# Windowed attention on one core: four score banks filled in one block, one value block, transposed probabilities in the scores' banks

## Chip, core and metric

The kernel runs on one core of a Trainium2 chip. The metric is the device time of one execution in microseconds, median of several runs. Engines: TensorE (PE, with its weight loads PEld), VectorE (DVE), ScalarE (ACT), GpSimd (POOL), and SP, which here only issues transfers.

## What is computed

A decoder layer on x of 4 x 512 tokens x 256, in float32: a gated recurrence, a mixing block over a context, and then two layers of local attention with an MLP. The change touches only the attention:

```python
h = shift_token(x)                      # second half of the features from the token before
q, k, v = split(h @ wqkv, 3)            # 8 heads of 64
q, k = rotary_xpos(l2norm(q) * qs, l2norm(k) * ksc)
sim = einsum('bhwid,bhwjd->bhwij', q * 8, [k of window before, k of own window])   # windows of 128 tokens
attn = softmax(where(mask, -max, sim))
x = x + (attn @ v) @ wo                 # then the MLP with GELU, x = x + ...
```

There are two such layers, over four sequences (batches) of 512 tokens, each of four windows. In a batch the first window has no window before it, so its keys are 128 wide and not 256.

## The kernel before, in words

The attention of a layer is a loop over 16 windows (tiles of 128 tokens), four to a batch, w = 0 to 3 their place in the batch. The loop body holds the windows w = 1, 2, 3 and the w = 0 of the next batch; the first window stands ahead of the loop, the last three behind it. It is software-pipelined by hand: while window n has its scores taken, window n - 1 is finished (prev), the keys and queries of n + 1 are transposed (one), the projections of n + 2 run (two), and the input of n + 3 is transposed (three). Each engine runs its own program in order; the only ties are semaphore waits (`wait_ge`), and the order within each engine's `window` function is the schedule.

On TensorE (`window`, L1847) the order before is: scores of head pairs 0 and 1 (`score_pairs(n, w, 0)`, L1798), transposes of the reciprocal row sums of n - 1 (L1836), projection 0 of n + 2 (queries, `qkv`, in `product`, L1509), value weighting of pairs 2 and 3 of n - 1 (L1825), scores of pairs 2 and 3, projection 1 (keys), transposes of the probabilities of pairs 0 and 1 (L1810), output projection of n - 1 (`project_o`, L1844), value weighting of pairs 0 and 1 of n, key transposes of n + 1 (L1777), projection 2 (values), query transposes (L1784), probability transposes 2, input transposes (L1754), probability transposes 3. A head pair fills the 128 rows of the array: its two heads' scores are matmuls over 64 rows each, and its two heads' values are matmuls into 64 columns each. A float32 matmul stands as two records in the trace, so four of them are "x8".

On VectorE (L986): `masked` 0 and 1 (add mask, take row maxima, L957; then the row bias, L963), rope of projection 0 (L926, L931), `normalise` (writes o_t of n - 1, L978), `norm_keys` (L946), `masked` 2 and 3, `att_residual` (adds the output projection of n - 1 into the stream, L984), rope of projection 1, reciprocal of the sums, sum of squares, low part of the input. On ScalarE (L1394): copy of the transposed row sums (L1392), square of projection 0 (L1342), exponentials of pairs 0 and 1 (L1370), square of projection 1, copies of the transposed probabilities 0 and 1 (`probs_transposed`, L1381, at w = 0 L1384), exponentials 2, key copy, exponentials 3, query copy, input copy, probability copies 2, value copy, probability copy 3.

PSUM has eight banks. Banks 0 and 1 hold projections, 2 the transposes of keys, queries and sums and the output projection, 3 the weighted values, 4 and 5 the transposed probabilities (pair i in 4 + i % 2), 6 and 7 the scores (one bank for each head of a pair, two pairs side by side). Semaphores that matter: `c_qk` (scores done), `c_tt` (maxima taken, scores read), `c_ex` (exponentials), `c_pt` (probabilities transposed), `c_pt_out` (copied out), `c_pv` (values weighted), `c_ot_out` (o_t written), `c_wo` (output projected), `c_res` (added). `transpose_k` of n + 1 writes bank 2 and so waits for `c_res` of n - 1. `probs_t` holds two pairs. `w_stage` is the landing buffer of weights, whole for the attention's weights and its first 1068 columns for the MLP's.

Of the kernel before, what the change touches and what calls it, by code (L numbers as in the profile page):

```python
# [25 lines left out]
P = 128  # L26
# [23 lines left out]
W1_GROUPS = 2 * KH - 1  # L50
BAND = 64
# [17 lines left out]
def build(nc, x, ctx_in, cols_in, rows_in, w_in, w_gate, w_out, wq, wk, wv, wo_x, pos_bias,  # L69
          w1_x, w2_x, lcols_in, qk_scale, rope, wqkv, wo_l, wm_l, out):  # L70
    with ExitStack() as ctx:
# [130 lines left out]
        probs_t = sb("probs_t", [P, 2, 4, P], stack=st_att)  # L202
        st_att.close()
# [58 lines left out]
        def _(sp):  # L262
# [28 lines left out]
            def load_att(l):  # L291
                sp.dma_start(w_stage[:, :], wqkv[l].rearrange("p k n -> p (k n)")).then_inc(wqkv_in, 16)
                if l:
                    sp.wait_ge(c_wo, l * NT)
                sp.dma_start(wo_sb[:, :, :], wo_l[l]).then_inc(wo_in, 16)
# [311 lines left out]
        def _(dve):  # L607
# [341 lines left out]
            def masked(n, w, i, first=False):  # L949

                u = 4 * n + i
                nk = 2 * P if w else P
                if not (isinstance(u, int) and u < 2):
                    dve.wait_ge(c_ex, 2 * u - 2)
                wait_alone(dve, c_qk, 2 * n + i // 2 + 1)
                for e in range(2):
                    dve.tensor_tensor_reduce(scores[:, i % 2, e, 0:nk],  # L957
                                             bank[6 + e][:, (i % 2) * 2 * P:(i % 2) * 2 * P + nk],
                                             mask[:, 2 * P - nk:2 * P], 1.0, NEG, ALU.add, ALU.max,
                                             row_max[:, w % 2, 2 * i + e:2 * i + e + 1]).then_inc(c_tt, 1)  # L960
# [208 lines left out]
        def _(act):  # L1169
# [204 lines left out]
            def probs_transposed(n, w, i):  # L1374

                u = 4 * n + i
                act.wait_ge(c_pt, u + 1)
                if not (isinstance(n, int) and n == 0 and i < 2):
                    act.wait_ge(c_pv, 2 * n + i // 2)
                if w:  # L1380
                    act.activation(probs_t[:, i % 2, :, :], bank[4 + i % 2][:, :].rearrange("p (c t) -> p c t", t=P),  # L1381
                                   ACT.Copy).then_inc(c_pt_out, 1)
                else:
                    act.activation(probs_t[:, i % 2, 0:4:2, :],  # L1384
                                   bank[4 + i % 2][:, :].rearrange("p (c t) -> p c t", t=P)[:, 0:4:2, :],
                                   ACT.Copy).then_inc(c_pt_out, 1)
# [118 lines left out]
        def _(pe):  # L1505
# [281 lines left out]
            def score_pairs(n, w, g):  # L1787

                if g == 0:
                    pe.wait_ge(c_qt, n + 1)  # L1790
                if not (isinstance(n, int) and n == 0 and g == 0):
                    pe.wait_ge(c_tt, 8 * n + 4 * g)
                k0 = max(w - 1, 0) * P
                nk = (w + 1) * P - k0
                for i in (2 * g, 2 * g + 1):
                    for e in range(2):
                        half = slice(e * DH, (e + 1) * DH)
                        ins = pe.matmul(bank[6 + e][:, (i % 2) * 2 * P:(i % 2) * 2 * P + nk], q_t[half, i, :],  # L1798
                                        k_t[half, i, k0:(w + 1) * P], start=True, stop=True)
                ins.then_inc(c_qk, 1)  # L1800

            def transpose_probs(n, w, i):
# [3 lines left out]
                if not (isinstance(n, int) and n == 0 and i < 2):  # L1806
                    pe.wait_ge(c_pt_out, u - 1)
                for e in range(2):
                    for k in range(2 if w else 1):
                        ins = pe.transpose(bank[4 + i % 2][:, (2 * e + k) * P:(2 * e + k + 1) * P],  # L1810
# [3 lines left out]
            def weigh_values(n, w, g):  # L1814

                pe.wait_ge(c_pt_out, 4 * n + 2 * g + 2)
                if g == 0:
                    pe.wait_ge(c_v, n + 1)
                    pe.wait_ge(c_ot_out, n)
                nk = 2 if w else 1  # L1820
                for i in (2 * g, 2 * g + 1):
                    for k in range(nk):
                        for e in range(2):
# [3 lines left out]
                                            probs_t[:, i % 2, 2 * e + k, :], start=(k == 0), stop=(k == nk - 1))  # L1827
# [19 lines left out]
            def window(n, w, l, prev, one, two, three):  # L1847
                score_pairs(n, w, 0)
                if prev:
                    transpose_sums(n - 1)  # L1850
                if two:
                    qkv(n + 2, (w + 2) % TT, 0)
                if prev:
                    weigh_values(n - 1, (w - 1) % TT, 1)
                score_pairs(n, w, 1)
                if two:
# [5 lines left out]
                weigh_values(n, w, 0)  # L1862
# [103 lines left out]
            for l in range(LAYERS):  # L1966
# [14 lines left out]
                weigh_values(n0 + NT - 1, TT - 1, 1)  # L1981
# [88 lines left out]
```

## Times and profile before

| | us |
|---|---|
| median of 3 runs | 1061.69 |
| lowest, highest | 1060.79, 1063.59 |
| span of the profiled execution | 1063.7 |
| TensorE busy in it | 983.9 (92%) |
| VectorE, ScalarE, GpSimd busy | 697.0, 556.5, 398.4 |
| attention windows of layer 0 / layer 1 start at | 391.8 / 730.1 |
| the MLPs behind them start at | 614 / 949 |

The span is the time from the first to the last instruction of one execution. In the views a matmul's record begins at its start; the chain of waits sets its pieces 0.07 to 0.25 us later, since it reckons by the ends. A weight load overlaps the matmul before it.

### The profile page before, as it was taken

What the parts mean: (1) busy time and instruction counts of PE and PEld (TensorE: products, weight loads), DVE (VectorE), ACT (ScalarE), POOL (GpSimd) and SP (SyncE); (2) the same over time, 40 slices, a digit from 0 to 9 for tenths busy, and PEclk for the clock granted to TensorE, in tenths of its full rate; (3) what the DMA queues carried; (4) which work ended last, traced back from release to release, by engine and by line L of the source; (5) the groups of instructions that cost most, each with busy time, mean ns of one, the idle gap of its engine ahead of it and who ended that gap; (6) DMA issues with size and microseconds to landing.
All of it is one profiled execution on the core that took longest, in us unless ns stands there. A gap on an engine that the chain in (4) does not pass through costs nothing.

```text
span 1063.7 us, 18012 instructions
## 1 busy us (share of the span) xinstructions
PE 983.9 (92%) x5720; PEld 777.0 (73%) x5720; DVE 697.0 (66%) x1814; ACT 556.5 (52%) x1217; POOL 398.4 (37%) x417
## 2 busy tenths in 40 slices
PE   5889969999999979999999799998999999989987
PEld 4768855777676857777777588886777777768876
DVE  6888476366575677777778545575777777735563
ACT  4467721404030327777777734444777777754432
POOL 4232613113130366666666300115565656510030
PEclk9889979999999999999999999999999999989999
DMA  6101012000000000000001110000000000000010
GB/s 244 64 1 60 20 40 104 1 1 0 0 0 1 1 21 2 2 22 0 21 0 32 41 60 9 0 21 1 2 22 0 21 0 24 17 12 10 1 55 25
DMA packets 14349, 25.38 MB, mean 24 GB/s; under 512 B 864, under 2 KB 11224, under 8 KB 13528
## 3 DMA queue, kind: packets, MB, share of 16 engines
q1 hardware_dynamic: 14296, 24.72, 6.9%
q8 instruction: 27, 0.44, 0.2%
q14 instruction: 26, 0.21, 0.1%
HBM read 20.53 MB, written 2.10 MB: 21 GB/s over the span
## 4 chain that ended last, share of the span: by engine, by line
PE 74%; DVE 12%; issue 6%; ACT 4%; POOL 3%; DMA 0%; POOLq 0%; DVEq 0%; ACTq 0%
PE bank L1509 32%; PE bank L1704 5%; PE bank L1798 5%; PE bank L1656 5%; PE bank L1844 5%; PE bank L1825 4%; PE bank L1917 4%; PE bank L1810 4%; PE bank L1777 2%; PE bank L1836 2%; PE bank L1667 1%; PE bank L1784 1%; DVE scores L957 1%; POOL scanned L376 1%; PE bank L1575 1%
## 5 line engine op out<-in xcount | busy, mean ns | idle before, releaser
L1370 ACT ACTIVATE probs<-scores,row_bias,q_rnorm 128x256 f32<-128x256 f32 (+1 forms) x256 | 143.7, 565 | 10.7 <-DVE row_bias L963 10.1
L957 DVE CUSTOM_DVE_ANT_0 scores<-bank,mask 128x256 f32<-128x256 f32 (+1 forms) x256 | 89.2, 385 | 20.5 <-PE bank L1798 16.1
L507 POOL TENSOR_TENSOR norms<-norms,minus_half 128x16 f32<-128x16 f32 x32 | 93.6, 2925 | 2.7
L1509 PE MATMUL bank<-wqkv_hi,x_hi 128*128 128x512 f32 x192 | 85.4, 445 | 2.5 <-DVE rot L931 1.4
L490 POOL TENSOR_TENSOR k_tok<-rot 128x512 f32<-128x512 f32 x32 | 41.2, 1287 | 101.0 <-DVE rot L931 101.0
L1509 PE MATMUL bank<-wqkv_hi,x_lo 128*128 128x512 f32 x192 | 77.0, 401 | 0.0
L1509 PE MATMUL bank<-wqkv_lo,x_hi 128*128 128x512 f32 x192 | 77.0, 401 | 0.0
L1102 DVE SCALAR_TENSOR_TENSOR hidden<-bank,lcols,hidden 128x512 f32<-128x512 f32 (+1 forms) x48 | 35.9, 749 | 60.9 <-PE bank L1509 52.8
L1798 PE MATMUL bank<-k_t,q_t 64*128 64x256 f32 (+1 forms) x512 | 66.1, 377 | 10.1 <-DVE row_max L957 8.6
L1810 PE MATMUL bank<-ident,probs 128*128 128x128 f32 x448 | 65.9, 274 | 5.2 <-ACT probs L1370 5.0
L1342 ACT ACTIVATE squares<-bank 128x512 f32<-128x512 f32 x64 | 38.3, 598 | 61.1 <-PE bank L1509 61.1
L1825 PE MATMUL bank<-probs_t,v_tok 128*64 128x128 f32 x896 | 65.2, 286 | 1.3 <-ACT probs_t L1384 1.3
L1825 PEld LDWEIGHTS bank<-probs_t,v_tok 128*64 128x64 f32 x896 | 49.3, 140 | 22.6 <-issue 20.8
L1844 PE MATMUL bank<-wo_sb,o_t 128*128 128x256 f32 x256 | 64.2, 396 | 1.7 <-DVE o_t L978 1.7
L1509 PE MATMUL bank<-t_hi,wm_hi 128*128 128x512 f32 x160 | 64.3, 402 | 0.0
L1509 PE MATMUL bank<-t_lo,wm_hi 128*128 128x512 f32 x160 | 63.6, 397 | 0.0
L1509 PE MATMUL bank<-t_hi,wm_lo 128*128 128x512 f32 x160 | 62.7, 392 | 0.0
L1810 PEld LDWEIGHTS bank<-ident,probs 128*128 128x128 f32 x448 | 52.2, 141 | 13.0 <-ACT probs L1370 7.8
L1798 PEld LDWEIGHTS bank<-k_t,q_t 64*128 64x128 f32 x512 | 41.7, 186 | 24.6 <-DVE row_max L957 11.0
L490 POOL TENSOR_TENSOR q_tok<-rot 128x512 f32<-128x512 f32 x32 | 46.7, 1459 | 33.1 <-DVE rot L931 33.1
L926 DVE TENSOR_TENSOR rot<-bank,rope_l 128x512 f32<-128x512 f32 x64 | 44.0, 687 | 23.0 <-ACT squares L1342 22.8
L1704 PE MATMUL bank<-w,ff 128*128 128x256 f32 x256 | 56.7, 379 | 0.0
(242 smaller groups left out, 2620.0 us busy)
## 6 DMA issues: line engine op xcount, KB each, us to landing
w_stage<-in_wm_l_dram SPq DMA_DIRECT2D x8, 534.0 KB, 3.5
w_stage<-in_wqkv_dram SPq DMA_DIRECT2D x2, 1536.0 KB, 7.4
out_dram<-stream SPq DMA_DIRECT2D x4, 512.0 KB, 2.9
emb<-in_ctx_dram SPq DMA_DIRECT2D x1, 1536.0 KB, 6.5
inner<-in_w_gate_dram SPq DMA_DIRECT2D x1, 1152.0 KB, 9.1
stream<-in_x_dram SPq DMA_DIRECT2D x2, 512.0 KB, 5.1
stream<-in_x_dram SPq DMA_DIRECT2D x1, 1024.0 KB, 11.5
ew<-in_pos_bias_dram SPq DMA_DIRECT2D x1, 1024.0 KB, 11.2
```

Of the source, the lines that this page charges most:

```text
L490: pool.tensor_tensor(dst[:, par, :], rot[:, 2 * i, :], rot[:, 2 * i + 1, :], ALU.add)\
L507: pool.tensor_tensor(norms[:, 2, :], norms[:, 1, :], minus_half[:, :], ALU.pow).then_inc(c_rn, 1)
L926: dve.tensor_tensor(rot[:, 2 * i, :].rearrange("p (h d) -> p h d", d=DH), src, cos, ALU.mult)\
L957: dve.tensor_tensor_reduce(scores[:, i % 2, e, 0:nk], bank[6 + e][:, (i % 2) * 2 * P:(i % 2) * 2 * P + nk], mask[:, 2 * P - nk:2 * P], 1.0 ...
L1370: act.activation(probs[:, i % 2, e, 0:nk], scores[:, i % 2, e, 0:nk], ACT.Exp, bias=row_bias[:, w % 2, h:h + 1], scale=q_rnorm[:, w, h:h + 1],
L1509: ins = pe.matmul(out, stationary, moving, start=(first and i == 0), stop=(last and i == len(terms) - 1))
L1656: ins = pe.matmul(bank[2 + (2 * m + i + 2) % 4][:, :], src[:, j, m * P:(m + 1) * P], ew_t[:, j, :], start=(j == 0), stop=(j == TT - 1))
L1704: ins = pe.matmul(bank[6 + t // 2][:, (t % 2) * D:(t % 2 + 1) * D], ff[:, k, t * P:(t + 1) * P], w_2[:, k, :], start=(k == 0), stop=(k == ...
L1798: ins = pe.matmul(bank[6 + e][:, (i % 2) * 2 * P:(i % 2) * 2 * P + nk], q_t[half, i, :], k_t[half, i, k0:(w + 1) * P], start=True, stop=True)
L1810: ins = pe.transpose(bank[4 + i % 2][:, (2 * e + k) * P:(2 * e + k + 1) * P], probs[:, i % 2, e, k * P:(k + 1) * P], ident[:, :])
L1825: ins = pe.matmul(bank[3][e * DH:(e + 1) * DH, i * P:(i + 1) * P], v_tok[:, w - nk + 1 + k, h * DH:(h + 1) * DH], probs_t[:, i % 2, 2 * e ...
L1844: ins = pe.matmul(bank[2][:, 0:D], o_t[:, k, :], wo_sb[:, k, :], start=(k == 0), stop=(k == KI - 1))
```

## The change

`score_pairs` takes all four head pairs in one block, pairs 0 and 1 into banks 6 and 7, pairs 2 and 3 into banks 4 and 5. The transposed probabilities of a pair go to one of the banks from which its scores have been read, so a scores bank is free again when ScalarE has copied them out. The value weighting of a window is one block of all four pairs, and stands in the next window behind the transposes of the row sums. `probs_t` is four deep; its second half lies in `w_stage` from column 2048 on. Projections 0 and 1 follow each other on TensorE, and ScalarE's square of projection 0 stands behind the exponentials of pairs 0 and 1. SP waits for the last value weighting before it loads `w_stage` again.

```diff
+SCORES = (6, 4)
+        probs_t_far = w_stage[:, 2 * KD * INNER:4 * KD * INNER // 2 + 2 * 4 * P].rearrange(
+            "p (i c t) -> p i c t", i=2, t=P)
+        probs_ts = [(probs_t, probs_t_far)[i // 2][:, i % 2, :, :] for i in range(KI)]
...
             def load_att(l):
+                if l:
+                    sp.wait_ge(c_pv, l * NT)
...
             def normalise(n):
-                dve.wait_ge(c_pv, 2 * n + 2)
+                dve.wait_ge(c_pv, n + 1)
...
             def probs_transposed(n, w, i):
-                if not (isinstance(n, int) and n == 0 and i < 2):
-                    act.wait_ge(c_pv, 2 * n + i // 2)
+                if not (isinstance(n, int) and n == 0):
+                    act.wait_ge(c_pv, n)
...
             def window(n, w, l, prev, one, two, three):      # ScalarE
-                if two:
-                    square(n + 2, 0)
                 exps(n, w, 0)
                 exps(n, w, 1)
                 if two:
+                    square(n + 2, 0)
                     square(n + 2, 1)
...
+            def score_pairs(n, w):
+                pe.wait_ge(c_qt, n + 1)
...
+                for i in range(KI):
+                    if i % 2 == 0 and not (isinstance(n, int) and n == 0):
+                        pe.wait_ge(c_pt_out, 4 * n - 2 + i)
...
             def transpose_probs(n, w, i):
                 pe.wait_ge(c_ex, 2 * u + 2)
-                if not (isinstance(n, int) and n == 0 and i < 2):
-                    pe.wait_ge(c_pt_out, u - 1)
+                pe.wait_ge(c_tt, 8 * n + 4 * (i // 2) + 4)
...
+            def weigh_values(n, w):
+                pe.wait_ge(c_pt_out, 4 * n + 4)
+                pe.wait_ge(c_v, n + 1)
+                pe.wait_ge(c_ot_out, n)
...
             def window(n, w, l, prev, one, two, three):      # TensorE
-                score_pairs(n, w, 0)
+                score_pairs(n, w)
                 if prev:
                     transpose_sums(n - 1)
+                    weigh_values(n - 1, (w - 1) % TT)
                 if two:
                     qkv(n + 2, (w + 2) % TT, 0)
-                if prev:
-                    weigh_values(n - 1, (w - 1) % TT, 1)
-                score_pairs(n, w, 1)
-                if two:
                     qkv(n + 2, (w + 2) % TT, 1)
                 transpose_probs(n, w, 0)
                 transpose_probs(n, w, 1)
                 if prev:
                     project_o(n - 1)
-                weigh_values(n, w, 0)
                 if one:
                     transpose_k(n + 1, (w + 1) % 2, [(c_res, n)] if prev else [])
```

## Rows read from the trace of the kernel before

**Rows 1.** The page: granted clock in 40 slices, and one transfer.
```profile
PEclk9889979999999999999999999999999999989999
...
w_stage<-in_wqkv_dram SPq DMA_DIRECT2D x2, 1536.0 KB, 7.4
```
**Rows 2.** By stretches: us, then busy time by engine, clock, DMA.
```profile
391.83:399.80 7.97, 4.51 (x24) 2.98 (x23) 5.89 (x26) 2.28 (x7) 7.63 (x7) 0.75 0.00 0
...
407.79:421.20 13.41, 13.41 (x97) 10.52 (x97) 10.36 (x33) 10.30 (x29) 7.00 (x7) 1.00 0.00 1
421.20:435.08 13.88, 13.88 (x105) 10.94 (x104) 10.02 (x33) 10.47 (x29) 8.77 (x9) 1.00 0.01 3
448.97:461.13 12.16, 11.97 (x89) 9.34 (x89) 9.40 (x33) 9.00 (x28) 8.78 (x9) 1.00 0.14 47
...
592.83:602.50 9.67, 7.83 (x70) 5.77 (x69) 7.54 (x29) 6.22 (x17) 1.71 (x3) 1.00 0.03 9
```
**Rows 3.** The chain that ended last: start, length, what (a w = 2 window).
```profile
421.27 1.06 PE bank L1798 x8
422.33 0.59 PE bank L1836 x4
...
424.33 1.02 PE bank L1825 x16
...
426.42 1.60 PE bank L1509 x6
428.01 0.87 PE bank L1810 x8
428.89 1.73 PE bank L1844 x8
...
431.64 0.59 PE bank L1777 x4
432.23 1.40 PE bank L1509 x6
433.62 0.44 PE bank L1784 x4
...
457.87 0.66 PE bank L1777 x4
...
464.23 0.59 PE bank L1825 x8
```
**Rows 4.** TensorE's timeline, cut inside the block: start, us, what.
```profile
421.52 0.60 PE L1798 MATMUL bank<-k_t,q_t 64*128 64x256 f32 x4
421.73 0.38 PE L1798 MATMUL bank<-k_t,q_t 64*128 64x256 f32 x2
...
428.72 1.89 PE L1844 MATMUL bank<-wo_sb,o_t 128*128 128x256 f32 x8
```
**Rows 5.** ScalarE's timeline: start, us, what.
```profile
422.10 0.62 ACT L1381 ACTIVATE probs_t<-bank 128x512 f32<-128x512 f32 x1
...
424.36 0.60 ACT L1342 ACTIVATE squares<-bank 128x512 f32<-128x512 f32 x1 [0.81 <-PE bank L1509]
...
426.61 0.59 ACT L1370 ACTIVATE probs<-scores,row_bias,q_rnorm 128x256 f32<-128x256 f32 x1
...
461.90 0.42 ACT L1384 ACTIVATE probs_t<-bank 128x256 f32<-128x256 f32 x1
```
**Rows 6.** VectorE's timeline: start, us, what.
```profile
426.35 0.68 DVE L978 TENSOR_TENSOR o_t<-bank,rsum_t 128x512 f32<-128x512 f32 x1
...
427.79 0.41 DVE L957 CUSTOM_DVE_ANT_0 scores<-bank,mask 128x256 f32<-128x256 f32 x1
...
429.74 0.16 DVE L963 SCALAR_TENSOR_TENSOR row_bias<-row_max,q_rnorm 128x2 f32<-128x2 f32 x1
...
455.23 0.28 DVE L957 CUSTOM_DVE_ANT_0 scores<-bank,mask 128x128 f32<-128x128 f32 x1
...
457.39 0.42 DVE L984 TENSOR_TENSOR inner<-inner,bank 128x256 f32 x1
```

More of the change, by code:

```diff
@@ L957, in masked @@
                     dve.tensor_tensor_reduce(scores[:, i % 2, e, 0:nk],
-                                             bank[6 + e][:, (i % 2) * 2 * P:(i % 2) * 2 * P + nk],
+                                             bank[SCORES[i // 2] + e][:, (i % 2) * 2 * P:(i % 2) * 2 * P + nk],
                                              mask[:, 2 * P - nk:2 * P], 1.0, NEG, ALU.add, ALU.max,
@@ L1376, in probs_transposed @@
                 u = 4 * n + i
+                src = bank[SCORES[i // 2] + i % 2][:, :].rearrange("p (c t) -> p c t", t=P)
                 act.wait_ge(c_pt, u + 1)
-                if not (isinstance(n, int) and n == 0 and i < 2):
-                    act.wait_ge(c_pv, 2 * n + i // 2)
+                if not (isinstance(n, int) and n == 0):
+                    act.wait_ge(c_pv, n)
                 if w:
-                    act.activation(probs_t[:, i % 2, :, :], bank[4 + i % 2][:, :].rearrange("p (c t) -> p c t", t=P),
-                                   ACT.Copy).then_inc(c_pt_out, 1)
-                else:
-                    act.activation(probs_t[:, i % 2, 0:4:2, :],
-                                   bank[4 + i % 2][:, :].rearrange("p (c t) -> p c t", t=P)[:, 0:4:2, :],
-                                   ACT.Copy).then_inc(c_pt_out, 1)
+                    act.activation(probs_ts[i], src, ACT.Copy).then_inc(c_pt_out, 1)
+                else:
+                    act.activation(probs_ts[i][:, 0:4:2, :], src[:, 0:4:2, :], ACT.Copy).then_inc(c_pt_out, 1)
             def sums_transposed(n):
@@ L1785, in transpose_q @@
                 ins.then_inc(c_t, 1)
[L1787 to L1792, printed above, removed]
+            def score_pairs(n, w):
+                pe.wait_ge(c_qt, n + 1)
                 k0 = max(w - 1, 0) * P
                 nk = (w + 1) * P - k0
-                for i in (2 * g, 2 * g + 1):
+                for i in range(KI):
+                    if i % 2 == 0 and not (isinstance(n, int) and n == 0):
+                        pe.wait_ge(c_pt_out, 4 * n - 2 + i)
                     for e in range(2):
                         half = slice(e * DH, (e + 1) * DH)
-                        ins = pe.matmul(bank[6 + e][:, (i % 2) * 2 * P:(i % 2) * 2 * P + nk], q_t[half, i, :],
-                                        k_t[half, i, k0:(w + 1) * P], start=True, stop=True)
-                ins.then_inc(c_qk, 1)
+                        ins = pe.matmul(bank[SCORES[i // 2] + e][:, (i % 2) * 2 * P:(i % 2) * 2 * P + nk],
+                                        q_t[half, i, :], k_t[half, i, k0:(w + 1) * P], start=True, stop=True)
+                    if i % 2:
+                        ins.then_inc(c_qk, 1)
             def transpose_probs(n, w, i):
@@ L1805, in transpose_probs @@
                 pe.wait_ge(c_ex, 2 * u + 2)
-                if not (isinstance(n, int) and n == 0 and i < 2):
-                    pe.wait_ge(c_pt_out, u - 1)
+                pe.wait_ge(c_tt, 8 * n + 4 * (i // 2) + 4)
                 for e in range(2):
                     for k in range(2 if w else 1):
-                        ins = pe.transpose(bank[4 + i % 2][:, (2 * e + k) * P:(2 * e + k + 1) * P],
+                        ins = pe.transpose(bank[SCORES[i // 2] + i % 2][:, (2 * e + k) * P:(2 * e + k + 1) * P],
                                            probs[:, i % 2, e, k * P:(k + 1) * P], ident[:, :])
                 ins.then_inc(c_pt, 1)
[L1814 to L1819, printed above, removed]
+            def weigh_values(n, w):
+                pe.wait_ge(c_pt_out, 4 * n + 4)
+                pe.wait_ge(c_v, n + 1)
+                pe.wait_ge(c_ot_out, n)
                 nk = 2 if w else 1
-                for i in (2 * g, 2 * g + 1):
+                for i in range(KI):
                     for k in range(nk):
@@ L1826, in weigh_values @@
                                             v_tok[:, w - nk + 1 + k, h * DH:(h + 1) * DH],
-                                            probs_t[:, i % 2, 2 * e + k, :], start=(k == 0), stop=(k == nk - 1))
+                                            probs_ts[i][:, 2 * e + k, :], start=(k == 0), stop=(k == nk - 1))
                 ins.then_inc(c_pv, 1)
@@ L1980, in _ @@
                 transpose_sums(n0 + NT - 1, True)
-                weigh_values(n0 + NT - 1, TT - 1, 1)
+                weigh_values(n0 + NT - 1, TT - 1)
                 project_o(n0 + NT - 1)
```

## The prediction

> **What bounds the kernel now.** I read the page first: TensorE is granted nearly its full clock through the attention slices [rows 1]. Then the view by stretches, one attention window at a time. A window is one 128-token tile, and 32 of them run, 16 per layer. In the first window of a batch of the loop (w = 1) TensorE is busy 13.41 of 13.41 us, in the next two 13.88 of 13.88, in the last (w = 0) 11.97 of 12.16 [rows 2]. VectorE and ScalarE are busy 9 to 10.5 us of the same windows [rows 2]. So the attention loop is bound by TensorE, in program order, and every other engine has three to four microseconds of slack, but their work comes in a chain with due times, and slack in the total doesn't say that a link is in time. The chain of waits confirms it: the window that starts at 421.27 is TensorE blocks laid end to end, with no other engine between them [rows 3]. Last I read the timelines of ScalarE and VectorE for when their links in that window are done [rows 5, 6]; a reorder on a full engine is decided by those times.
>
> **What the change removes on TensorE.** Scores and value weighting use half of the array's rows or columns. Entering and leaving such a block costs: the block behind one is longer than the same block behind a full-array one, transposes 0.59 against 0.44 and a projection 1.60 against 1.40 [rows 3]. Inside a scores block the second pair of matmuls starts at 421.52, 0.32 us after the first, the third at 421.73, only 0.21 after the second [rows 2, 4]. Before there are four such blocks per window in three places; after there are two.
> Scores: one block of 1.06, and four more pairs at 0.215 = 0.86, so 1.92 for 2.12. Value weighting: 16 records take 1.02 and 8 take 0.59, so 8 more cost 0.43, and 32 cost 1.02 + 2 x 0.43 = 1.88 for 2.04. The key transposes now follow a full-array block: 0.44 for 0.59. The two projections still are one of 1.60 and one of 1.40. Sum: -0.20 - 0.16 - 0.15 = **-0.50 us per window**, in the 26 windows that TensorE bounds -13 us.
> The Trainium skill (TensorEngine Tiling, Key Properties) says that changing the tiling mode drains the engine; the rows agree in kind. Its page "TensorE: Matmul & The Clock Gate" (Step-by-step, the drain) gives some 128 cycles for a drain, 53 ns at 2.4 GHz; three changes of mode fewer would by that estimate be 0.16 us per window, -4 us in all, where the rows above give -13.
>
> **What the change adds: three waits on TensorE.** I lay the new order along a window's clock, zero at its first scores matmul (421.20), with the lengths of [rows 3, 4]. A chain piece lies 0.07 behind the matmul's own start, so a block started from a wait takes 0.07 more (0.66 for the transposes at 457.87, 0.59 behind a running block).
> *First wait.* Pairs 2 and 3 now write banks 4 and 5, where the transposed probabilities of the window before lie, and wait for `c_pt_out` of its last copy. ScalarE ends that copy at 422.72 [rows 5], 1.52 into the window; it is the tail of a ScalarE queue that starts with the query copy, which the change doesn't touch. With 0.06 for the handover (an end at 457.81 releases TensorE at 457.87 [rows 3, 6]) the second half starts at 1.58 and ends at 2.71, where it would have ended at 1.99: **+0.72**. Queued behind it on TensorE is everything.
> *Second wait.* Row-sum transposes to 3.30, the value block to 5.18, the first projection to 6.78. Only then can ScalarE square it; the move of `square(n + 2, 0)` behind `exps` costs nothing by itself, for the four exponentials, 0.58 apart, are done by 6.2. Before, the square began at 3.16 (424.36) [rows 5]. VectorE's queue runs from that square to rope to `normalise`: o_t starts 1.99 behind the square's start [rows 5, 6], so at 8.80, ends 0.68 later and releases `project_o` at 9.54. TensorE is there after the second projection (1.40) and the transposes (0.87), and would end the product at 10.78; from the wait it takes 1.89 [rows 4] and ends at 11.43: **+0.65**.
> *Third wait.* Behind `project_o` stood `weigh_values(n, w, 0)`, 1.02 us, which hid the residual addition; now `transpose_k` follows at once and waits for `c_res`. `att_residual` stands in VectorE's queue behind `masked` 2 and 3, which stand behind `normalise`: masked 2 starts 1.44 behind o_t (427.79 against 426.35), the last row bias 1.95 later, the addition 0.13 behind that and takes 0.42 [rows 6]. That is 10.24, 12.19, 12.32 and 12.74, so `transpose_k` starts at 12.80 and not at 11.43, and ends at 13.46 instead of 11.87: **+1.59**.
> The rest (1.40, 0.44, 0.44, 0.22, 0.44) leads to 16.40, 16.33 for the start of the next scores. ScalarE's tail hangs on the query transposes as before, so its last copy again ends 1.5 into the next window: the waits repeat and nothing catches up. A window with w = 2 or 3 takes 16.33 for 13.88, **+2.45** (-0.50 + 0.72 + 0.65 + 1.59).
> *w = 1*, by the same steps: the last copy is half as long and ends at 462.32, 1.19 in [rows 5]; the value block is 16 records; the exponentials (from 3.5) end at 5.84 and set the square. o_t 7.83, `project_o` from 8.57 to 10.46, the addition done at 11.77, next window at 15.36 for 13.41: **+1.95**. *w = 0*: scores at half width (0.65), value block still 1.88, o_t at 8.39, `project_o` to 11.02, masked 2 at 9.81, the addition 2.16 behind it (455.23 to 457.39 [rows 6]), next window at 15.6 for 12.16: **+3.45**.
> **Sum.** A batch of four windows +1.95 + 2 x 2.45 + 3.45 = 10.3, six batches in both loops 61.8. The window w = 1 behind each loop, two in all, 3.9. In the last two windows of a layer VectorE's MLP preparation is late already; I take +0.25 each layer for w = 2 and nothing for w = 3, whose saved value block (1.02) is paid again in the doubled block behind it. The first window of a layer has no previous tile and no third wait and loses a 0.59 block: I take -1.2, with 0 and -2.5 as ends. Together 61.8 + 3.9 + 0.5 - 2.4 = **+63.8**.
> **Edits at no cost.** `load_att(1)` waits for `c_pv` before w_stage is loaded again. On SP's queue the output weights' load behind it and two shifts wait for `c_wo` in any case, which comes after `c_pv`; the staged weights are first used in the last MLP batch, tens of microseconds later. Without that cover it would cost its own 7.4 us, once [rows 1]. POOL's rope additions shift with VectorE's rope and still end ahead of their users. The transposes' new wait for `c_tt` is for maxima taken 2 us and more earlier.
> The trace doesn't show the new waits; each is bounded from below by what is structural. The first lies between 0.4 (the w = 1 copy) and 0.8. The second is between 0 (VectorE wholly in time) and 1.1 (its size in w = 0). The third is at least 0.65 (an addition of 0.42, two handovers, and the slower start from a wait) and at most 1.8. I take the values of the walk, which lie nearest to rows of the same window.
>
> **How it stands to the median.** The profiled execution spans 1063.7 us, 0.2% over the median 1061.69. So 1063.7 + 63.8 is 1127.5 there and **1125 us** for the median, 6% slower.
>
> **Rivals.**
> *The waits are covered (faster).* For it: all three fed engines are busy under 10.5 of 13.88 us. Without a wait `project_o` would be due at 8.33 (1.99 + 0.59 + 1.88 + 1.60 + 1.40 + 0.87) and `transpose_k` at 10.06. If o_t were done by 8.27 and the addition by 10.0, -0.50 x 26 would stand alone: 1048. From those two points on it is slower, and against it speaks that o_t ends 2.67 behind the start of the square, so the square would have to start by 5.60, while the projection that it reads ends at 6.06 at the earliest.
> *Only the structural waits stay.* If VectorE's masks 2 and 3 don't delay the addition, a window pays 0.72 + 0.65 - 0.50 = 0.87, over 28 windows +24: 1086. Against it: the queue order is fixed in the code.
> *The clock falls too.* TensorE's share in a window would be 13.4 of 16.33, 82%. The slowed last window of a layer has 7.83 of 9.67, 81%, at a granted clock of 1.00 [rows 2], which speaks against it. For it: in the layer's first window, with TensorE 57% busy, 7.97 us run at a mean of 0.75 [rows 2], a loss of 2.0. One such stretch in each of eight batches is 16 more, 1141; one in each of 26 windows 52 more, 1177.
> *The edit does not do what it says.* If TensorE's pairs didn't run closer in one long block, the 0.50 goes and the waits stay: 1138, inside the range.
>
> **How the numbers follow.** Forecast 0.70 (1105 to 1145, by the bounds of the waits), structural waits alone 0.12, clock 0.08, a gain 0.06, and 0.04 for an outcome between these last and no change. The range 1085 to 1150 takes in the first two and the milder clock case. A difference of 0.3% (3.2 us) is about what a measurement of this kernel can tell. Faster 0.06, same 0.02, slower 0.92.
>
> **What would show it.** In the chain of waits the windows should no longer be TensorE alone: ScalarE's probs_t copy ahead of the second half of the scores, o_t ahead of the output projection, and the residual addition ahead of the key transposes, the last the largest. Scores matmuls 2 and 3 should start 1.6 us behind the first. The window should be 16.3 and its TensorE work 13.4. Windows of 13.4 without gaps would refute it; gaps with a clock below 0.95 in the middle of the loop would be the clock's.

## The result, and the profile after

| | before | after |
|---|---|---|
| median, us | 1062.12 (1060.79 to 1063.59) | 1129.93 (1129.12 to 1130.78) |
| ratio to before | | 1.0637 [1.0622, 1.0652] |
| profiled execution's span, us | 1063.7 | 1127.4 |
| mean granted clock | 0.975 | 0.984 |

The change makes the kernel 6.4% slower, 67.8 us in the medians and 63.7 in the spans (the profiled execution of before lies 1.6 above its median, that of after 2.5 below). The forecast was 1125.

The page of after first, since it says in three lines what has changed. Section 1 is busy time by engine, section 2's line the granted clock in 40 slices, section 4 the chain that ended last, by engine.

```profile
PE 977.2 (87%) x5720; PEld 774.1 (69%) x5720; DVE 701.2 (62%) x1814; ACT 556.4 (49%) x1217; POOL 390.7 (35%) x417
...
PEclk9899899999999989999999999999999999999999
...
PE 56%; DVE 20%; ACT 10%; issue 9%; POOL 3%; DVEq 1%; DMA 0%; POOLq 0%; ACTq 0%
```

Every engine does the work that it did before. What is new is that TensorE is now only 56% of the chain, for 74% in the kernel before, and VectorE and ScalarE are 30% of it, for 16%. The clock line answers to that of [rows 1]: the 8 near its end, at the end of the second layer's attention, is gone, and behind the slice with the first windows (395 to 423 us) nothing is below 9.

The second reading is the groups of TensorE with their idle time (busy us, mean ns of one, idle before and who ended it). Each of the three lines is one wait.

```profile
L1845 PE MATMUL bank<-wo_sb,o_t 128*128 128x256 f32 x256 | 63.4, 390 | 18.7 <-DVE o_t L984 18.7
...
L1800 PE MATMUL bank<-k_t,q_t 64*128 64x256 f32 (+1 forms) x512 | 64.8, 374 | 13.3 <-ACT w_stage L1388 10.9
...
L1780 PE MATMUL bank<-ident,k_tok 128*128 128x128 f32 x128 | 21.3, 290 | 45.9 <-DVE inner L990 42.6
```

The output projection waits for o_t, the scores for the copy of the transposed probabilities (their far half lies in w_stage), and the key transposes for the residual addition, by far the longest of the three. Then the chain of one window. It is the one that begins at 421.61, w = 2, the one whose forecast stands on [rows 3]: start, length, what.

```profile
422.71 0.50 ACT w_stage L1388
...
423.26 1.14 PE bank L1800 x8
...
424.98 1.90 PE bank L1826 x32
426.88 1.60 PE bank L1512 x6
...
428.50 0.61 ACT squares L1348
...
430.57 0.60 DVE o_t L984
431.17 1.39 DVE k_tok L952
432.56 0.33 DVE scores L963
...
434.48 0.43 DVE inner L990
...
434.96 0.66 PE bank L1780 x4
```

Where [rows 3] were TensorE blocks end to end, the chain now leaves TensorE for 0.5 us at the head of the window, and from 428.48 to 434.96, where it runs through the square, rope, o_t, the keys' normalisation, two masks and the residual addition. TensorE isn't idle for all of that: it has the second projection, the probability transposes and `project_o` beside it. By stretches (us, busy time by engine, clock, DMA), windows with w = 1, 2 and 0, against [rows 2]:

```profile
405.85:421.61 15.76, 13.22 (x88) 10.23 (x88) 10.49 (x33) 10.12 (x28) 7.39 (x8) 1.00 0.01 1
421.61:438.41 16.80, 14.06 (x105) 11.09 (x104) 10.33 (x33) 10.61 (x28) 8.33 (x9) 1.00 0.01 1
...
455.18:470.77 15.59, 12.53 (x98) 9.90 (x96) 9.20 (x33) 9.12 (x28) 8.35 (x9) 1.00 0.12 37
```

The clock stays at 1.00, and a window is 2.5 to 3.1 us longer than TensorE's busy time in it. Summed from the first scores matmul of each window to that of the next, the attention windows take 72.0 us more (37.1 in layer 0, 34.9 in layer 1); the stretch from the last window of layer 0 to the first of layer 1 takes 3.5 less (133.8 for 137.3), the rest behind the last window 2.7 less, and the first scores start 2.1 sooner. That is 63.7, the difference of the spans.

### The profile page after: what moved, and what is told of

Read it like the earlier page. It is cut to its first block, busy times and chain, and to the rows that moved or that the text cites. A ratio compares the mean times of both kernels' runs of the same rounds, so it can differ in the third digit from the quotient of the medians.

```text
span 1127.4 us, 17962 instructions
## 1 busy us (share of the span) xinstructions
PE 977.2 (87%) x5720; PEld 774.1 (69%) x5720; DVE 701.2 (62%) x1814; ACT 556.4 (49%) x1217; POOL 390.7 (35%) x417
## 4 chain that ended last, share of the span: by engine, by line
PE 56%; DVE 20%; ACT 10%; issue 9%; POOL 3%; DVEq 1%; DMA 0%; POOLq 0%; ACTq 0%
PE bank L1512 26%; PE bank L1707 5%; PE bank L1659 5%; PE bank L1914 4%; PE bank L1826 3%; DVE k_tok L952 3%; DVE scores L963 3%; ACT probs L1376 3%; PE bank L1800 3%; PE bank L1780 2%; DVE o_t L984 2%; ACT squares L1348 2%; ACT v_tok L1353 1%; DVE rot L937 1%; PE bank L1837 1%
## 5 line engine op out<-in xcount | busy, mean ns | idle before, releaser
L1512 PE MATMUL bank<-wqkv_hi,x_hi 128*128 128x512 f32 x192 | 82.3, 428 | 2.2 <-DVE rot L937 1.4
L496 POOL TENSOR_TENSOR q_tok<-rot 128x512 f32<-128x512 f32 x32 | 41.0, 1282 | 105.1 <-DVE rot L937 105.1
L1800 PE MATMUL bank<-k_t,q_t 64*128 64x256 f32 (+1 forms) x512 | 64.8, 374 | 13.3 <-ACT w_stage L1388 10.9
L1845 PEld LDWEIGHTS bank<-wo_sb,o_t 128*128 128x128 f32 x256 | 46.0, 190 | 30.3 <-DVE o_t L984 25.4
L1780 PE MATMUL bank<-ident,k_tok 128*128 128x128 f32 x128 | 21.3, 290 | 45.9 <-DVE inner L990 42.6
```

The source lines that it names most:

```text
L496: pool.tensor_tensor(dst[:, par, :], rot[:, 2 * i, :], rot[:, 2 * i + 1, :], ALU.add)\
L1512: ins = pe.matmul(out, stationary, moving, start=(first and i == 0), stop=(last and i == len(terms) - 1))
L1800: ins = pe.matmul(bank[SCORES[i // 2] + e][:, (i % 2) * 2 * P:(i % 2) * 2 * P + nk], q_t[half, i, :], k_t[half, i, k0:(w + 1) * P], start= ...
L1845: ins = pe.matmul(bank[2][:, 0:D], o_t[:, k, :], wo_sb[:, k, :], start=(k == 0), stop=(k == KI - 1))
```

## The experiments

All but the last are the kernel after with the order of a few calls changed and nothing of its computation left out. Ratios are to the kernel before. "Window" is the distance between the first scores matmuls of two windows, w = 2 and 3 unless it says otherwise: 16.8 us in the kernel after.

**The first wait, alone.** ScalarE's values copy stood between the last two probability copies.

```diff
                 probs_transposed(n, w, 2)
+                probs_transposed(n, w, 3)
                 if two:
                     values(n + 2, (w + 2) % TT)
-                probs_transposed(n, w, 3)
```

> The kernel after, with one edit: ScalarE copies the last transposed probabilities before the values, so that copy ends 0.48 us earlier (one 128x512 copy behind another). Theory of three waits: the wait of the second half of the scores (0.8 us in the trace of after) falls by 0.48 in nearly all of 30 windows, and since everything behind it on TensorE follows without slack, the time falls by 13 to 14 us, to about 1116. Rival, that the window's pace is set by VectorE's queue as a whole and a wait taken away in one place comes back in the next: the output product and the key transposes wait 0.48 longer, and the time stays at 1130.

Measured: 1118.54 us (1115.96 to 1121.04), 1.0529 [1.0508, 1.0550]. The window fell to 16.3. TensorE's timeline shows the scores as one block again (start, us, what):

```profile
434.99 2.22 PE L1800 MATMUL bank<-k_t,q_t 64*128 64x256 f32 x16
```

11 of the 68 us hung on one ScalarE copy of 0.6 us in the wrong place, where 13 to 14 were expected. In this profile the stretch behind the second layer's last window is 2.2 us longer than in that of after (135.4 for 133.2), and 3.4 us of it (992.2 to 995.6) run at a granted clock of 0.50. The block is still 2.2 and not the 1.9 of my sum; two probability copies remain behind the query copy.

**The second wait, alone.** Projection 0 goes ahead of the value block on TensorE, and its square ahead of the exponentials on ScalarE.

```diff
                     transpose_sums(n - 1)
-                    weigh_values(n - 1, (w - 1) % TT)
                 if two:
                     qkv(n + 2, (w + 2) % TT, 0)
+                if prev:
+                    weigh_values(n - 1, (w - 1) % TT)
+                if two:
                     qkv(n + 2, (w + 2) % TT, 1)
...
+                if two:
+                    square(n + 2, 0)
                 exps(n, w, 0)
                 exps(n, w, 1)
                 if two:
-                    square(n + 2, 0)
                     square(n + 2, 1)
```

> The kernel after, with projection 0 ahead of the value block on TensorE and its square ahead of the exponentials on ScalarE, as before the change; the blocks stay whole. Theory: the square starts at about 4.9 us into the window and not at 6.9, o_t is done by 7.6, ahead of the output product, so the second wait (0.65 us) goes, and the masks and the addition come 1.9 us earlier, so that the third falls to 0.6. The window goes from 16.8 to 14.9, the time to about 1080. Rival, that the exponentials, now later by 2 us, hold up the probability transposes instead: these would wait, and the gain is under half, above 1105.

Measured: 1084.31 us, 1.0201 [1.0184, 1.0219]; window 14.9, as expected, the time 4 us above what was expected. This one move takes back 46 of the 68 us, more than the second term of my sum, because VectorE's whole queue starts from that square and the third wait hangs on the same queue. The chain of a window here:

```profile
419.94 1.39 PE bank L1513 x6
421.33 1.90 PE bank L1827 x32
...
424.80 0.87 PE bank L1813 x8
425.67 1.74 PE bank L1846 x8
...
427.56 0.43 DVE inner L990
...
428.03 0.66 PE bank L1781 x4
```

`project_o` follows the probability transposes with no wait. The key transposes start 0.62 behind it, with the addition alone between them: the structural part of the third wait, for which I had 0.65.

**The third wait, from VectorE's side.** Masks 2 and 3 go ahead of rope, so that nothing but the keys' normalisation stands between o_t and the addition.

```diff
                 masked(n, w, 1)
+                masked(n, w, 2)
+                masked(n, w, 3)
                 if two:
                     rope_products(n + 2, (w + 2) % TT, 0)
...
                     norm_keys(n + 1, (w + 1) % 2)
-                masked(n, w, 2)
-                masked(n, w, 3)
```

> The kernel after, with VectorE's masks 2 and 3 moved ahead of the rope of projection 0, into the 4.3 us that it idles there. Theory: the third wait is mostly the two masks standing between o_t and the residual addition. The addition then starts when the output product ends (11.6 us into the window) and not at 12.87, the key transposes start at 12.1 and not at 13.35: 1.2 us less in each of 26 to 28 windows, 32 us in all, to about 1098; the wait left ahead of the key transposes is 0.6 to 0.7. Rival, that the addition is late because the output product itself is late: no change of the time, under 5 us.

Measured: 1115.69 us, 1.0485 [1.0463, 1.0507], 14 us below after, under half of the 32 that were expected. The direction held, the size didn't. Windows w = 2, 3 fell by 1.1 us to 15.67, down to the same structural wait, the addition alone (chain):

```profile
433.06 2.01 PE bank L1845 x8
...
435.20 0.43 DVE inner L990
...
435.68 0.65 PE bank L1780 x4
```

But w = 0 and w = 1 gained only 0.6 and 0.5, and where VectorE has the MLP preparation to do the masks come at its cost: the final w = 2 window of each layer is 1.5 longer (13.58 for 12.08), and the stretch between the layers 2.8 longer (136.5 for 133.8). Not all of the 2.8 need be the masks': 3.4 us of that stretch (635.2 to 638.6) run at a granted clock of 0.50, which the kernel after doesn't have there, and behind the second layer, at full clock, the difference is 1.8.

**The third wait, from TensorE's side.** The last projection goes between `project_o` and the key transposes, as cover for the addition, and the query transposes behind the third probability transposes.

```diff
+                if two:
+                    qkv(n + 2, (w + 2) % TT, 2)
                 if one:
                     transpose_k(n + 1, (w + 1) % 2, [(c_res, n)] if prev else [])
...
-                if two:
-                    qkv(n + 2, (w + 2) % TT, 2)
+                transpose_probs(n, w, 2)
                 if one:
                     transpose_q(n + 1, (w + 1) % 2)
-                transpose_probs(n, w, 2)
```

> The kernel after, with projection 2 moved between the output product and the key transposes, and the query transposes behind probability transposes 2. Theory: the key transposes still wait for the residual addition and start where they did (13.35 us into the window), the 1.4 us of projection 2 are inside the wait; but the key copy and the exponentials of pair 3 behind it on ScalarE are no earlier, and hold up the last probability transposes, which gives most of it back: the window falls by 0.4 to 0.7 us, the time to 1112 to 1118. Rival, that TensorE's waits alone count and what is put into one is gained whole: 1.4 us in 26 windows, 36 us, to 1094.

Measured: 1121.35 us, 1.0548 [1.0510, 1.0585]; window 16.42, 0.37 less. The 1.4 us of cover is there and is nearly all given back, as the theory had it; the gain is still smaller than its 0.4 to 0.7 and the time above its 1112 to 1118. From the chain behind the key transposes:

```profile
434.44 0.43 DVE inner L990
...
434.92 0.67 PE bank L1780 x4
...
436.11 0.89 ACT probs L1376 x3
...
439.10 0.50 ACT w_stage L1388
```

The key transposes still start at the same point of the window, since the addition ends when it did. Behind them nothing is left that TensorE could do while ScalarE goes through its tail (key copy, exponentials, query copy, x, values, probabilities), so the next scores wait for that tail. The wait that was covered on TensorE came back where ScalarE's queue ends.

**Was the keys' normalisation slowed by GpSimd?** In the window above k_tok takes 1.47 us in its own record, and masked 2 starts 1.99 behind o_t where [rows 6] have 1.44. VectorE multiplies two SBUF operands there, while GpSimd adds q_tok. In a second profile of the kernel before the same place, w = 2, reads (VectorE's and GpSimd's timeline):

```profile
427.07 0.91 DVE L946 TENSOR_TENSOR k_tok<-k_tok,norms 128x512 f32<-128x512 f32 x1
```
```profile
427.39 1.74 POOL L490 TENSOR_TENSOR q_tok<-rot 128x512 f32<-128x512 f32 x1
```

There VectorE is first and GpSimd's addition is the one that is drawn out, 1.74 for some 1.27. In the kernel after it is the other way:

```profile
430.74 1.27 POOL L496 TENSOR_TENSOR q_tok<-rot 128x512 f32<-128x512 f32 x1 [3.00 <-DVE rot L937]
```
```profile
431.08 1.47 DVE L952 TENSOR_TENSOR k_tok<-k_tok,norms 128x512 f32<-128x512 f32 x1
```

The change of order between the two engines is one of w = 2, 3 and 0. In w = 1 GpSimd was first before the change too (413.29), and VectorE drawn out. In w = 0 it was another VectorE instruction that started inside GpSimd's addition, the row bias of masks 2 (128x2, else 0.16 us). The same second profile, w = 1 and then w = 0 on both engines:

```profile
413.63 1.50 DVE L946 TENSOR_TENSOR k_tok<-k_tok,norms 128x512 f32<-128x512 f32 x1
```
```profile
455.64 1.26 POOL L490 TENSOR_TENSOR q_tok<-rot 128x512 f32<-128x512 f32 x1
```
```profile
455.87 1.05 DVE L963 SCALAR_TENSOR_TENSOR row_bias<-row_max,q_rnorm 128x2 f32<-128x2 f32 x1
```

Moving the multiplication behind the masks takes it out of that overlap:

```diff
-                if one:
-                    norm_keys(n + 1, (w + 1) % 2)
                 masked(n, w, 2)
                 masked(n, w, 3)
+                if one:
+                    norm_keys(n + 1, (w + 1) % 2)
                 if prev:
                     att_residual(n - 1, t - 1)
```

> The kernel after, with VectorE's norm_keys behind masks 2 and 3 and ahead of the residual addition. In the trace of after this product of two SBUF operands takes 1.47 us; it starts 0.34 us after GpSimd's q_tok addition and ends 0.5 us after that ends. Theory: it is held up by GpSimd's addition, alone it takes 0.68. Moved, it runs when GpSimd is idle and takes 0.68, the addition starts 0.75 us earlier in each window, and the time falls by about 20 us, to 1109. Rival, that 1.47 is what it costs wherever it stands in this order: 1.4 us again and the time stays within 5 us of 1130.

Measured: 1114.63 us, 1.0481 [1.0463, 1.0499], 15 us less where some 20 were expected; window 15.95, 0.84 less, w = 1 and w = 0 0.7 and 0.6 less; the first windows of the layers lose 2.6 and 2.4 of that again, since there the later keys are what the transposes wait for, and in the second 3.4 us (763.2 to 766.6) run at a granted clock of 0.50, which the kernel after doesn't have there. The same 32 instructions in the kernel after, grouped by form (duration ns min/median/max):

```profile
L952 DVE TENSOR_TENSOR k_tok<-k_tok,norms x32: 681/1473/1477, 382.5 to 987.8; 128x512 f32<-128x512 f32 x32
```

and in this one:

```profile
L952 DVE TENSOR_TENSOR k_tok<-k_tok,norms x32: 691/692/721, 383.3 to 976.3; 128x512 f32<-128x512 f32 x32
```

And the two engines' timelines in it:

```profile
433.37 1.27 POOL L496 TENSOR_TENSOR q_tok<-rot 128x512 f32<-128x512 f32 x1 [3.00 <-DVE rot L937]
```
```profile
433.72 0.41 DVE L963 CUSTOM_DVE_ANT_0 scores<-bank,mask 128x256 f32<-128x256 f32 x1
...
435.68 0.69 DVE L952 TENSOR_TENSOR k_tok<-k_tok,norms 128x512 f32<-128x512 f32 x1
```

Beside the same GpSimd addition (1.27 us) the masks, which read a PSUM bank, keep their 0.41, and the multiplication behind it takes 0.69. So in the kernel after 0.78 us of a k_tok was lost to GpSimd and no work; 26 of the 32 took 1.38 us or more there, and 8 of 32 in the kernel before. The Trainium skill ("SBUF — State Buffer", Who interferes with whom) says that a VectorE instruction with two SBUF inputs and a GpSimd instruction that reads SBUF contend for a port pair, and that the one issued second is blocked altogether. By that rule whichever starts second is drawn out, and the rows agree: GpSimd's 1.74 before, VectorE's 1.47 after, and the row bias's 1.05, which ends when GpSimd's addition does. VectorE's 0.91 before isn't free of it either: a GpSimd copy of 0.41 us (x_tile) had started 0.04 us ahead of it. From these rows the loss is the time that the two overlap less some 0.12 to 0.15 us: 0.78 of 0.93, 0.89 of 1.03, 0.22 of 0.37, and 0.47 of 0.59 on GpSimd's side.

**Can the blocks' gain be had without the waits?** This kernel joins three of the edits above (values behind the last probability copy, projection 0 and its square early, projection 2 as cover), and the tail of the window rearranged on both engines:

```diff
 # ScalarE, behind the first two probability copies
                 exps(n, w, 2)
+                exps(n, w, 3)
                 if one:
                     keys(n + 1, (w + 1) % TT)
...
-                exps(n, w, 3)
+                probs_transposed(n, w, 2)
                 if one:
                     queries(n + 1)
+                probs_transposed(n, w, 3)
                 if three:
                     x_transposed(n + 3, (w + 3) % TT, bank[1][:, 0:D])
-                probs_transposed(n, w, 2)
                 if two:
                     values(n + 2, (w + 2) % TT)
-                probs_transposed(n, w, 3)
 # TensorE, behind the key transposes
                 transpose_probs(n, w, 2)
                 if one:
                     transpose_q(n + 1, (w + 1) % 2)
+                transpose_probs(n, w, 3)
                 if three:
                     transpose_x(n + 3, (w + 3) % 2, bank[1][:, 0:D], [(c_rope, 6 * (n + 2) + 6)])
-                transpose_probs(n, w, 3)
```

> The kernel after, with all its blocks and banks, and the order mended in all places: values copied last, projection 0 and its square early, projection 2 ahead of the key transposes, exponentials 2 and 3 together ahead of the key copy, each late copy behind its transposes. Theory: the three waits are under 0.3 us together, and the 0.50 us that the whole blocks save stands: the window is 13.4 to 13.8, the time 1045 to 1062. Rival, that the blocks save nothing and the reorder only restores the earlier schedule: 13.9 and 1062 or more.

Measured: 1054.09 us (1051.52 to 1056.35), 0.9919 [0.9890, 0.9949]: faster than the kernel before by 0.8%. One window of it in the chain:

```profile
486.42 2.00 PE bank L1801 x16
...
489.01 1.37 PE bank L1513 x6
490.38 1.90 PE bank L1827 x32
...
497.85 0.45 PE bank L1781 x4
498.32 0.61 ACT k_t L1358
...
498.98 0.66 PE bank L1788 x4
```

All three waits of the change are gone. The scores are one block of 2.00 (1.93 behind a running block), the value weighting 1.90, the key transposes 0.45, as the sum had them (1.92, 1.88, 0.44). The time is inside the 1045 to 1062 of the theory, the window isn't: 14.0 for 13.4 to 13.8, and the rival had 13.9. What keeps it there, 0.1 above before, is a new wait of 0.68 (from the transposes' end at 498.30 to 498.98): the query transposes wait for ScalarE's key copy. TensorE's own blocks add up to 13.3, so the 0.5 us was there and was spent. The windows up to each layer's last take 1.7 us more than before in all (w = 0 takes 12.7 for 12.15), so the net gain over before comes from the layers' ends: the stretch between the layers (131.9 for 137.3) and the one behind the last window (130.9 for 135.9). A part of it is the clock, below: the kernel after has 133.8 and 133.2 there. Another candidate is that in this order the last window's exponentials go ahead of ScalarE's scaling for the MLP (`mlp_scaled`). No run has this order with the blocks of before, so it isn't shown that the whole blocks gain anything.

**Two tries at that last wait.** The row-sum transposes ahead of the scores, as cover for the last query copy:

```diff
-                score_pairs(n, w)
                 if prev:
                     transpose_sums(n - 1)
+                score_pairs(n, w)
```

> As the reordered kernel, with the row-sum transposes ahead of the scores block, which gives the last probability copy 0.44 us more before the scores need its bank. Theory: what is left of the first wait (0.1 to 0.3 us) goes and the window is 13.4 to 13.5: 1045 to 1052, at most 8 us faster than the reordered one. Rival: the maxima start 0.44 later and with them VectorE's queue, and a wait of that size shows ahead of the output product or the transposes of the probabilities: no faster than the reordered one.

Measured: 1060.94 us, 0.9988 [0.9966, 1.0009]; window 14.2. The theory fell, and the time came out as the rival had it, but not by the rival's path: no wait shows ahead of the output product or the transposes of the probabilities. The wait for the key copy lies elsewhere in the window and stays, and the projection behind the scores pays for leaving a half-array block, 1.60 for 1.37. Then, in this kernel and in the one before it, the last two probability transposes ahead of the query transposes, so that they lie in the wait:

```diff
                 transpose_probs(n, w, 2)
+                transpose_probs(n, w, 3)
                 if one:
                     transpose_q(n + 1, (w + 1) % 2)
-                transpose_probs(n, w, 3)
```

> As x7_sums_first, with the last two probability transposes ahead of the query transposes, so that TensorE has 0.45 us of work while ScalarE copies the transposed keys. Theory (the wait for the key copy is what the steady windows lose): that wait falls from about 0.7 us to 0.25, and windows w = 2, 3 go from 14.2 to about 13.8 us, w = 0 from 12.85 to 12.4, some 8 to 11 us in all, about 1051 us. Rival: ScalarE, which now copies the queries later, is what the first scores wait for; then the wait only moves and the time stays within 3 us of x7's 1061 us.

> As x6_reordered, with the same one move: the last two probability transposes ahead of the query transposes. Theory: the wait for the key copy shrinks by the 0.45 us of the block now in it, less what the scores then wait for the query copy (0.15 to 0.4 us); windows w = 2, 3 from 14.0 to about 13.85, some 3 to 5 us in all, about 1050 us. Rival: the scores wait for the query copy as long as the block was, and the time stays within 2 us of x6's 1054 us.

Measured: 1060.89 us, 0.9977 [0.9964, 0.9991], and 1054.87 us, 0.9922 [0.9907, 0.9937]. The windows are those of the kernels without the move, 14.2 and 14.0, and both rivals hold. The chain of the second:

```profile
486.04 0.48 PE bank L1788 x4
...
486.55 0.61 ACT q_t L1364
...
487.28 2.00 PE bank L1801 x16
```

The wait for the key copy is gone and one of 0.76 for the query copy has taken its place, ahead of the scores. In each of these four orders one ScalarE copy of 0.6 us stays on the path between the last transposes and their first reader. How to take that away too stays open.

**The clock at the layers' ends, in a second profile of the kernel before.**

> The kernel before, unchanged, for a second profile. Question: in the first profile the granted clock is at its lower level for about 7 us near the end of each layer's attention, in all profiles of the changed order there for 3.4 us or less. If that is a property of the order of work, the same stretches show the lower level again, and the stretch from the last window of layer 0 to the first of layer 1 takes 137.3 us again. If it was chance, the low stretches lie elsewhere or are gone, and that stretch takes about 134 us.

It took 1063.8 us of span, with the same stretch between the layers, 137.27. In slices of 3.4 us across the end of layer 0 (columns as above):

```profile
603.40:606.80 3.40, 1.41 (x11) 0.93 (x9) 0.20 (x1) 3.13 (x8) 0.51 (x1) 1.00 0.01 2
606.80:610.20 3.40, 2.47 (x20) 1.90 (x20) 2.38 (x3) 3.27 (x5) 3.21 (x8) 0.63 0.24 54
610.20:613.60 3.40, 3.33 (x9) 2.67 (x9) 0.02 (x1) 0.00 (x0) 0.00 (x0) 0.50 0.95 398
```

and the kernel after across the same point of its run:

```profile
637.40:640.80 3.40, 1.25 (x10) 0.77 (x8) 0.20 (x1) 3.14 (x8) 0.81 (x2) 1.00 0.02 5
640.80:644.20 3.40, 2.55 (x37) 2.14 (x37) 2.44 (x3) 2.98 (x5) 2.91 (x7) 1.00 0.01 2
644.20:647.60 3.40, 3.40 (x16) 2.88 (x17) 0.42 (x1) 0.12 (x1) 0.00 (x0) 1.00 0.93 347
```

The output projection of the last tile, eight matmuls, runs at the lower level of the clock (0.50 is 1.2 GHz) before and takes 3.78 us in the chain of that profile, where the kernel after takes 1.99 at full clock. So the low stretch isn't chance alone: both profiles of before have it, some 7 us behind each layer, and the profile of the kernel after and that of the rearranged one don't. But the order doesn't settle it either. Three of the other changed orders have 3.4 us of it behind one of the two layers and none behind the other, and the stretch there is longer than in the kernel after: by 2.2 us with the early copy (second layer), by 2.8 with the early masks and by 1.6 with the cover (first layer). What I can't say is why the later order escapes it: TensorE is idle for much the same time ahead of it in both (busy 1.41 and 2.47 of 3.40 before, 1.25 and 2.55 after). That stays open.

## Why the prediction was right, and where it wasn't

**The sum.** Forecast 1125.0, measured 1129.93; +63.8 against a difference of 63.7 in the spans. The nearness is better than the terms deserve: the windows came out 8.2 above the sum and everything outside them 8.3 below it. That the two cancel is luck, and in the medians the difference was 67.8 for the 63.3 of the forecast.

**The blocks: right.** Scores 1.93 to 2.00 for 1.92, value block 1.90 for 1.88, key transposes 0.44 to 0.45 where no wait stands ahead of them.

**First wait: right in kind and size.** The second half of the scores starts 1.65 into the window (423.26 − 421.61); the walk had 1.58. The first experiment takes most of it away and gives back 11 us.

**Second wait: right.** The square starts at 6.89, where the walk has the projection's end at 6.78; o_t at 8.88 for 8.80, `project_o` at 9.61 for 9.54.

**Third wait: the mechanism right, one term mis-sized.** The walk put the addition at 12.32; it starts at 12.87 (434.48). The step that failed is "masked 2 starts 1.44 behind o_t". It starts 1.99 behind, because the multiplication of k_tok in between takes 1.47. In the window of [rows 6] it started ahead of GpSimd's q_tok addition and took 0.91; the change makes GpSimd the first there. In w = 1 the trace of before had 1.49 already, so there the walk failed by carrying the 1.44 over from another window. I had written that GpSimd's additions "still end ahead of their users" and priced them at nothing, which is true for their users and beside the point: they also share something with VectorE. Per window that is 0.4 to 0.55, which turns the forecast 2.45 for w = 2 and 3 into the measured 2.9, and 1.95 for w = 1 into 2.35. In w = 0 the same delay is hidden by another error: the addition comes 1.47 after masked 2 (465.61 to 467.08) and not the 2.16 that I took, so 3.42 was measured for 3.45. The 2.16 had the same cause in it: the row bias of 1.05, which in the kernel after takes 0.16, since GpSimd is done by then. A batch of four windows gives 11.6 for 10.3, and six of them the +8 us over the forecast.

**The layers' ends: missed.** I took nothing for the stretch behind a layer's last window and argued about the clock only as something that could fall. It rose, and the two stretches came out 3.5 and 2.7 us shorter. Of that the last output product alone is 1.8 (1.99 for 3.78); how much of the rest is the clock's isn't separated. The row was before me, an 8 near the end of the clock line of [rows 1], and I didn't follow it to its place. Another 2 us of the cancelling is the start of the kernel, where the first scores begin at 389.8 for 391.8; over the kernels here that point lies anywhere from 387 to 392, so it is scatter and no effect.

**The smaller terms.** The w = 1 windows behind the loops +2.04 each (1.95), the final w = 2 +0.20 (0.25), the first windows +0.1 and −2.2, together −2.1 for −2.4. The −2.2 is that of layer 1, and there the kernel before ran 3.4 us (737.2 to 740.6) at a granted clock of 0.50 and the kernel after none, so that the total fits is luck as well.

**The rivals.** That the waits are covered fell, by the chain. "Only structural waits" fell too, but the experiment on the second wait is nearly this rival built: with the square early, the window pays 1.0 where the rival had 0.87, and the time is 1084 for its 1086. The clock didn't fall. The pairs do run closer in one long block. What makes the kernel slower is its order, not its blocks: with the order rearranged and the same blocks the kernel takes 0.8% less than before, though its windows take no less.

## What to carry to other kernels

On a kernel that one engine fills, a longer block of that engine's work is paid for by everyone whose input it delays: walk each of the other engines' queues from its new start, and look for the one instruction (here the square of projection 0) that starts a whole queue. Reorder the feeding engines together with the bound one: the same blocks go with 6.4% more time in one order and 0.8% less in another. And when queues shift against each other, ask of each pair that newly overlaps whether it shares a memory port, since a duration read from the trace of before holds only for the neighbours that it had there.

## What the runs showed of the hardware

- A VectorE multiplication of two SBUF operands, 128x512 f32, takes 0.69 us alone and 1.47 when it starts 0.34 us behind a GpSimd addition of 1.27 us on SBUF; a 128x2 row bias of 0.16 us took 1.05 in the same place; a mask pass that reads PSUM keeps its 0.41 beside the same addition.
- The lower level of TensorE's clock came at the same place in two profiles of the kernel before, and made eight matmuls take 3.78 us for 1.99.
- One long half-array block cost less than two short ones: 32 records of value weighting 1.90 us where 16 took 1.02, and a scores block of 16 records 1.93 to 2.00 where one of 8 took 1.06.
